# Ternary weights by one rounding and a sign, and the attention weights loaded after the second tile's x

## The reference, cut to what matters

```python
def _bitlinear(x, w_latent):
    scale = clip(mean(abs(w_latent), axis=1, keepdims=True), 1e-05, None)
    tern = clip(round(w_latent / scale), -1.0, 1.0)
    return x @ (tern * scale).T

h = _bitlinear(xn, w_fc) + gate * (xn @ v.T @ fast_b.T @ u.T)    # w_fc: 2048 x 512
r = maximum(h, 0.0)
ffn = _bitlinear(r * r, w_proj)                                  # w_proj: 512 x 2048
out = x + attention(xn, Wqkv, bqkv, Wout, bout) + ffn
```

## Time and profile before

| | |
|---|---|
| median of 3 runs | 2643.02 us (2641.61 to 2643.30) |
| the profiled execution | 2643.45 us, its span 2641.7 us |
| mean granted clock of TensorE | 0.986 |
| TensorE busy | 2580.7 us, 98% of the span |
| ScalarE busy | 1640.8 us, 62% |
| VectorE busy | 1600.3 us, 61% |
| GpSimd busy | 632.3 us, 24% |
| DMA | 167.43 MB, mean 63 GB/s |

### The profile page before, as it was taken

The page is one execution under the profiler, slowest core; times in us unless marked ns, Lnnn a source line. Parts: engine busy times, 40 slices in busy tenths (PEclk is TensorE's granted clock), DMA queues, the critical chain, the costliest instruction groups (busy, mean ns, idle before and its releaser), DMA issues.

```text
span 2641.7 us, 56009 instructions
## 1 busy us (share of the span) xinstructions
PE 2580.7 (98%) x19728; PEld 2093.2 (79%) x19728; DVE 1600.3 (61%) x4799; ACT 1640.8 (62%) x4260; POOL 632.3 (24%) x595
## 2 busy tenths in 40 slices
PE   5899999999999999989999999999999999999998
PEld 4688888888888888867888888888888888888885
DVE  6344444444444444347777777777777777777775
ACT  6333333333333333348888888888888888888885
POOL 0011111111111111033333333333333333333332
PEclk7999999999999999999999999999999999999998
DMA  4422222222222222021111111112111111112110
GB/s 168 157 80 80 80 79 79 79 79 79 79 79 79 79 79 64 33 80 34 33 54 45 42 57 42 57 33 66 33 52 46 42 57 42 57 33 63 35 49 26
DMA packets 188361, 167.43 MB, mean 63 GB/s; under 512 B 11328, under 2 KB 143424, under 8 KB 187632
## 3 DMA queue, kind: packets, MB, share of 16 engines
q1 hardware_dynamic: 188000, 164.41, 20.0%
q0 software_dynamic: 144, 0.17, 0.0%
HBM read 97.43 MB, written 67.11 MB: 62 GB/s over the span
## 4 chain that ended last, share of the span: by engine, by line
PE 55%; ACT 1%; issue 0%; DVE 0%; POOLq 0%; POOL 0%; ACTq 0%
PE pT_ps L1197 14%; PE job_ps L1109 14%; PE score_ps L1180 7%; PE job_ps L1221 7%; PE job_ps L1127 7%; PE job_ps L1118 7%; ACT wqkv_raw L932 0%; PE score_ps L1231 0%; ACT wqkv_raw L942 0%; PE job_ps L1241 0%; DVE k_lo L1042 0%; DVE wqkv_raw L1010 0%; ACT q_hi L958 0%; ACT k_hi L961 0%; POOLq L677 0%
## 5 line engine op out<-in xcount | busy, mean ns | idle before, releaser
L932 ACT ACTIVATE wqkv_raw<-wqkv_raw,neg_max 128x384 f32<-128x384 f32 (+1 forms) x1024 | 633.7, 619 | 186.5 <-DVE neg_max L1010 181.5
L892 POOL TENSOR_SCALAR wqkv_raw<-wqkv_raw,sum_rcp 128x384 f32<-128x384 f32 (+1 forms) x256 | 373.4, 1459 | 961.0 <-DVE sum_rcp L1021 961.0
L498 ACT ACTIVATE relu<-up_ps,fc_scale 128x512 f32<-128x512 f32 x256 | 176.4, 689 | 658.6 <-PE up_ps L629 658.6
L942 ACT COPY wqkv_raw<-pT_ps 128x384 f32<-128x384 f32 (+1 forms) x1024 | 485.3, 474 | 74.1 <-PE pT_ps L1197 73.5
L1197 PE MATMUL pT_ps<-ident,wqkv_raw 128*128 128x128 f32 x3040 | 514.2, 278 | 7.7 <-ACT wqkv_raw L942 7.7
L1010 DVE CUSTOM_DVE_ANT_0 wqkv_raw<-score_ps,mask 128x384 f32<-128x384 f32 (+1 forms) x1024 | 503.7, 549 | 5.3 <-PE score_ps L1180 1.6
L572 DVE SCALAR_TENSOR_TENSOR sq<-up_ps,relu 128x512 f32<-128x512 f32 x256 | 177.1, 692 | 530.7 <-ACT relu L498 530.3
L1197 PEld LDWEIGHTS pT_ps<-ident,wqkv_raw 128*128 128x128 f32 x3040 | 360.5, 140 | 119.1 <-ACT wqkv_raw L942 42.7
L639 PE MATMUL down_ps<-proj_T,sq_hi 128*128 128x512 f32 x1024 | 409.9, 400 | 7.0 <-DVE sq_lo L555 6.9
L641 PE MATMUL down_ps<-proj_T,sq_lo 128*128 128x512 f32 x1024 | 405.2, 396 | 0.0
L625 PE MATMUL up_ps<-f_xT_hi,fc_T 128*128 128x512 f32 x1024 | 399.7, 390 | 1.4 <-DVE low L543 1.4
(11 more groups left out here) (128 smaller groups left out, 4243.9 us busy)
## 6 DMA issues: line engine op xcount, KB each, us to landing
xT_hi<-xT SPq DMA_DIRECT2D x65, 256.0 KB, 3.7
xT_lo<-xT SPq DMA_DIRECT2D x65, 256.0 KB, 4.5
f_x_in<-in_L_attn_x SPq DMA_DIRECT2D x64, 256.0 KB, 3.3
xT<-f_xT_hi SPq DMA_DIRECT2D x64, 256.0 KB, 2.6
xT<-f_xT_lo SPq DMA_DIRECT2D x64, 256.0 KB, 2.8
part_in<-in_L_attn_x SPq DMA_DIRECT2D x64, 256.0 KB, 3.4
partial<-f_y SPq DMA_DIRECT2D x64, 256.0 KB, 2.0
wout_raw<-partial SPq DMA_DIRECT2D x64, 256.0 KB, 2.8
```

The lines of the kernel that those rows point to most:

```text
L892: nc.gpsimd.tensor_scalar(probs[:, u, cols], probs[:, u, cols], sum_rcp[:, u:u + 1], None, ALU.mult).then_inc(last_head_normalised, 1)
L932: nc.scalar.activation(probs[:, u, cols], probs[:, u, cols], ACT.Exp, bias=neg_max[:, u:u + 1], scale=-1.0, accum_out=prob_sum[:, u:u + 1] ...
L942: nc.scalar.copy(pT[:, h, first + seen.start:first + seen.stop, :].rearrange("p w t -> p (w t)"), pT_ps[:, h % 2, seen.start * P:seen.stop ...
```

## The change

In the preparation, clip_above is gone. round_ now multiplies by the reciprocal and adds the rounding constant in one instruction on VectorE, and so leaves the rounded quotient unclipped; it stands ahead of the next block's to_scale. The eviction on ScalarE takes Sign of the value less the constant instead of the value itself, which gives -1, 0 or 1. In the feed-forward stage SP issues the eight loads of attention's weights and biases in tile 0, after the loads of tile 1's x and of part_in, and ahead of the stores of tile 1's xT.

```diff
--- before.py
+++ after.py
@@ -118,7 +118,7 @@
             sem("f_ident_zeroed"), sem("f_ident_done"), sem("round_set"), sem("f_consts_set"))
 
         act_summed, proj_summed = sem("abs_summed_by_act"), sem("abs_summed_by_dve")
-        scale_done, inv_done, clipped, quantised = sem("scale_done"), sem("inv_done"), sem("clipped"), sem("quantised")
+        scale_done, inv_done, quantised = sem("scale_done"), sem("inv_done"), sem("quantised")
         turned, copied = sem("turned"), sem("copied")
         diag_done, scale_summed, low_summed, low_hi_done, prep_done = (
             sem("diag_done"), sem("scale_summed"), sem("low_summed"), sem("low_hi_done"), sem("prep_done"))
@@ -175,25 +175,20 @@
                 nc.vector.reciprocal(inv_scale[:, n:n + 1], scale[:, n:n + 1]).then_inc(inv_done, 1)
 
 
-            def clip_above(n):
+            def round_(n):
                 dve.wait_ge(inv_done, n + 1)
-                nc.vector.tensor_scalar(rows(n), rows(n), inv_scale[:, n:n + 1], 1.0, ALU.mult, ALU.min
-                                        ).then_inc(clipped, 1)
-
-            def round_(n):
-                dve.wait_ge(clipped, n + 1)
-                nc.vector.tensor_scalar(rows(n), rows(n), -1.0, ROUND, ALU.max, ALU.add).then_inc(quantised, 1)
+                nc.vector.tensor_scalar(rows(n), rows(n), inv_scale[:, n:n + 1], ROUND, ALU.mult, ALU.add
+                                        ).then_inc(quantised, 1)
 
 
             to_scale(0)
             invert(0)
             for n in range(FB + DC):
-                clip_above(n)
+                round_(n)
                 if 0 <= n + 1 - FB < DC and (n + 1 - FB) % 2 == 0:
                     sum_proj(n + 1 - FB)
                 if n + 1 < FB + DC:
                     to_scale(n + 1)
-                round_(n)
                 if n + 1 < FB + DC:
                     invert(n + 1)
                 if n == FB:
@@ -296,7 +291,7 @@
                 else:
                     c, g = divmod(n - FB, COLS)
                     dst = proj_T[:, g * 4:g * 4 + 4, c * P:(c + 1) * P]
-                nc.scalar.activation(dst, turn_ps[:, n % 4, :].rearrange("p (k t) -> p k t", k=4), ACT.Identity,
+                nc.scalar.activation(dst, turn_ps[:, n % 4, :].rearrange("p (k t) -> p k t", k=4), ACT.Sign,
                                      bias=neg_round[:, 0:1], scale=1.0).then_inc(copied, 1)
                 if n == FB:
                     act.wait_ge(low_summed, 1)
@@ -417,7 +412,6 @@
                                      xT[:, par, :, b * P:(b + 1) * P].bitcast(F32)).then_inc(xT_stored[b], 16)
 
             store_xT(0, 0)
-            weights.load(sp)
 
             def tile(i, par):
                 if not is_last(i):
@@ -429,6 +423,8 @@
                         sp.dma_start(block_rows(partial, NB * (i - 1) + b), y[:, b, :]).then_inc(stored[b], 16)
                 for b in range(NB):
                     sp.dma_start(part_in[:, b, :], block_rows(x, NB * i + b)).then_inc(part_here[b], 16)
+                if isinstance(i, int) and i == 0:
+                    weights.load(sp)
                 if not is_last(i):
                     store_xT(i + 1, 1 - par)
```

## The result

The changed kernel took 2627.67 us by the median of six runs (2625.78 to 2629.41), the kernel before 2642.38 by six runs taken with them (2640.08 to 2643.62). The medians are 14.7 us apart. The ratio of the times is 0.9946 with a 95% interval of 0.9933 to 0.9959, so the gain is 14.3 us by it, and 11 to 18 by the interval. The profiled execution took 2629.41 us against 2643.45, 14.0 less. The forecast was 2631.4 with a range from 2628.9: the direction and the place are as forecast, the time lies 1.2 us under the range.

The account below looks back on a forecast made before the run. TensorE, busy nearly throughout, bounds the kernel, so only its stalls before 90.9 us can pay. 2643.45 less 9.33 (move) and 2.34 (ternary part) gives 2631.8, less 0.43 to the median: 2631.4 us, range 2628.9 to 2635.2.

Parts of the forecast that it names:

- The move: Start of tile 1: x loads issued ahead of weights end TensorE's 6.87 us hole and 2.46 of low clock, 9.33 us.
- SP's cover: SP in tile 0: the moved loads end 2.3 us before the first store of tile 1's xT, so cost nothing.
- Sign at nothing: Preparation, ScalarE: 32 evictions as Sign cost what Identity costs, 0.69 us each; gain taken as 0.
- the single pass at the price of the first: Preparation, VectorE: one instruction per block at the old multiply's 0.49 or 1.28 us, saving 11.6 us of VectorE's time.
- The walk through the preparation: Preparation, from the 16th block on: steps followed through VectorE, TensorE and ScalarE gain 1.71 us, then 2.34 by its end.
- the last twelve evictions: End of preparation, ScalarE: run at its own pace, 0.596 us each, from 38.52 to 45.67, raising the gain to 2.34 us.
- the ternary part: Preparation: one VectorE instruction less in each of 20 blocks gains 2.34 us on the path, bounds 0 and 2.94.
- the clock: TensorE at tile 0: changed level timing taken as 0; up to 1.6 us saved if earlier, 2.46 lost if later.
- Only the move pays: Rival: the preparation ends no earlier, or a late clock at tile 0 takes its gain; 2633.8 us, chance 0.11.
- the table loads: ScalarE rivals: one more load, 2632.7 us, chance 0.05; about 29 switches in the preparation, 2663 us, chance 0.04.
- x in time: Tile 1's x lands before VectorE asks, over 3 us slack; rival that it doesn't: 2640.7 us, chance 0.04.
- The clock coming back late at tile 0: Tile 0, TensorE: late full clock takes the preparation's gain; part of a rival at 2633.8 us, chance 0.11.

Follow-up runs that it names:

- e8: Changed kernel with the five big weight loads put back ahead of tile 1's x, the three bias loads still after part_in; 2632.39 us, one run.
- e4: Changed kernel with Identity in place of Sign at the eviction, so the clip is left out and the output differs; median 2630.12 us, ratio 0.9955.
- e1: Kernel before with only the eight weight and bias loads moved, ternary weights made the old way; median 2627.75 us of five, ratio 0.9951.
- e3: Kernel before, both VectorE passes kept, only the rounding put ahead of the next block's scale; 2642.70 us, ratio 1.0003.
- e13: Changed kernel with 20 do-nothing VectorE instructions added in the preparation; 2629.60 us, one run.
- e14: Changed kernel with 8 do-nothing VectorE instructions added in the preparation; 2624.89 us, one run.
- e2: Changed kernel with the weight loads back in their old place, so only the ternary weights are new; 2638.76 us by 11 runs, ratio 0.9990.
- e5: The changed kernel itself, measured again; median 2630.63 us of five runs, ratio 0.9955.
- e10: Changed kernel with 10 unread TensorE products added at the last step of attention; median 2627.97 us, ratio 0.9946.
- e12: Changed kernel with later w_proj loads, tile 0's statistics made in the preparation, and unread TensorE products before tile 0 and at the end; 2619.68 us, ratio 0.9914.

## Why the prediction was right or wrong

- **The move, 9.33 us: right.** In the profile tile 1's first transposes go from 92.04 to 79.25; 3.46 of these 12.79 us come from the preparation, 9.33 from the hole. Over all profiles the hole is 50.47 to 50.67 with the loads ahead of x and 41.10 to 41.17 without (e8, with five of them ahead: 48.07). The price of the low clock behind the hole, 2.46, is in it. That the loads behind part_in cost nothing held too, though SP's cover was 0.55 us and not 2.3: the issues of the eight loads took 14.55 us and not 12.6, above all those of Wqkv, 4.42 instead of 3.03.
- **Sign at nothing: right** (e4), and the single pass at the price of the first (0.48 and 1.28): right.
- **The walk through the preparation: right up to the last twelve evictions.** From the data on, every start lies within 0.03 us of the forecast shifted by the 0.75 us of earlier data: the 16th block's pass 25.05, w_proj's first pass 28.16, the first eviction 30.65 (30.62), the last sum 35.80 (35.78). That data was 0.75 earlier in this profile is for the greater part chance: the eleven data starts of the new form lie within 1.25 us of one another. So the first bn_stats came at 48.73 and not 49.9, 0.75 earlier by the data and 0.37 by the evictions.
- **The term that was mis-sized: the ternary part.** I gave the last twelve evictions 7.15 us at ScalarE's own pace, and they take 6.83 or 6.84 in all 13 profiles of the new form. Part of this was a misreading: 5.36/9 takes in the tail of the last one, and from start to start the same rows give (48.01 - 42.82)/9 = 0.577 each, 6.92 for twelve. And I took the old ones from one profile, 7.75; in e1 and e3 they took 8.18 and 8.37. So the chain gives 2.71 (28.71 - 26.00) against that profile and 3.04 against the mean of the three old ones (29.04), not 2.34. On the other side stand 0.86 us that no step of mine had: the loss in the first pass of the loop (e13, e14). 9.33 + 3.04 - 0.86 = 11.51, against 11.67 forecast: two faults that nearly cancel, which is luck. With the data 0.26 earlier (23.10 in the mean of eleven profiles against 23.36 of three), if that is no chance, 11.77.
- **The step that failed: the clock and the range.** "I take 0" for the clock, with bounds for tile 0 only and 0.9 us for the spread of runs. The profiles show three places where it decides: tile 0 (lead 18.1 to 18.5, or 20.3), the passage (25.9 to 27.5) and the end (31.1 to 36.2). The profiled pair alone: 0.75 + 2.71 + 9.33 - 0.86, plus 0.90 at the passage and 1.19 at the end, = 14.02 of the 14.04 measured. The last two are no instruction of the change: they go with the mean clock (0.81 and 0.87 at the passage, 0.80 and 0.84 at the end), and kernels of both orders have had long and short ends. Then the reference: 2643.02 by three runs was 1.0 above the mean of 46. 2642.00 - 11.77 = 2630.2, and 11 runs of the changed kernel have a mean of 2629.05, five of e4, the same but for one function, a median of 2630.12. Six runs with a median of 2627.67 were, I take it, a favourable draw out of a spread that my range had no room for: single times of the changed kernel go from 2625.78 to 2630.86. Only one of the six left a trace, so for the others this is argued.
- **The rivals.** "Only the move pays" is out (e2), the table loads are out (one in the run), x in time is shown. The clock coming back late at tile 0 was in the first rival; it is real, but it falls on single runs of any of the kernels.

What stays open: the 1.2 us between 11.77 and the 12.95 of the means. Some 0.6 of it could be the passage, which took 26.75 to 27.18 (mean 27.0) in the three profiles with the old form and 25.94 to 27.49 (mean 26.4) in the 13 with the new. Its mean clock was 0.81 or 0.87; nothing was tried there. And why e5's five runs lie 2.5 us above the first six of the same kernel: the two profiles differ by 1.45, with 0.60 in the data, 0.28 in the passage and 0.75 in the end; for the other runs there is no trace. The groups ran on different chips, but the kernel before had means of 2642.2 and 2642.5 beside the two, so the chip alone explains little.

## What to carry to other kernels

A load that nobody needs soon should be issued behind one that somebody does, and what counts most is the bytes that it puts ahead, 6.9 of 9.3 us here, more than the issuing engine's time. When a pass is taken out of a chain, walk the chain from the last thing that does not move, here a landing: 11.6 us of VectorE's work were worth 3 here, and 0.86 of these were lost again in the first pass of the next loop. Where TensorE is starved, the clock makes the same code differ by microseconds from run to run: compare stretches in two profiles before a median of a few runs, and put that spread, measured at each starved place, into the range.

## What the runs showed of the hardware that I had not expected

- The issue of one DMA on SP took 0.88 us (qk_bias) or 0.65 (bout_wide) with the stores of xT ahead of it, and 4.16 and 4.53 with 4 MB of weights ahead.
- The end of the kernel took 31.1 to 36.2 us with the same instructions. It was 31.1 to 31.3 where TensorE's mean granted clock was 0.99 or 1.00, and 35.5 to 36.2 where it was 0.79 or 0.80. With ten products that nobody reads it took 31.2 in e10 and 32.9 in e12, but four profiles without them had 31.1 to 31.3 too.
- VectorE's first pass of the loop lost 0.86 us with 20 instructions fewer ahead of it (nine profiles), and none with 12 fewer, the old number, or 20 fewer and the statistics moved. Where it lost, an 8 KB packet of instructions was loaded within 0.4 us of the start of the slow one.
- Filling TensorE's idle time ahead of tile 0 made the stretch to the first relu 2.5 us shorter (15.93 against 18.46), though TensorE did more.
